# Graph attention layer: the residual's pass split in two and widened by the source terms, and the next graph's input norm one step sooner

## The reference, cut to what matters

```
h    = relu(layernorm(x))                         # input norm
Wh   = h @ W ;  src = Wh @ a[:64] ;  dst = Wh @ a[64:]
e    = leaky_relu(src[:, None] + dst[None, :], 0.2), masked where adj == 0
z    = elu(softmax(e) @ Wh + h @ W_res)           # residual term h @ W_res
out  = layernorm(z) * gamma + beta                # output norm
x    = x + out
```

## Time and profile before

| | us |
|---|---|
| median of 3 runs | 3389.66 |
| lowest, highest | 3387.86, 3393.14 |
| the profiled execution | 3394.82 |
| its span, first to last instruction | 3392.6 |

### The profile page before, as it was taken

How to read it: one execution, slowest core, us unless ns; L and a number is a source line. 1 busy time by engine, 2 the same in 40 slices (tenths; PEclk the granted TensorE clock), 3 DMA queues, 4 the chain that set the end, 5 groups by cost and what they waited for, 6 DMA issues and landing times. The chain is left out here.

```text
span 3392.6 us, 78775 instructions
## 1 busy us (share of the span) xinstructions
PE 3004.1 (89%) x30972; PEld 1659.6 (49%) x30972; DVE 3021.8 (89%) x4666; ACT 2922.6 (86%) x3806; POOL 994.7 (29%) x869
## 2 busy tenths in 40 slices
PE   7996999999999989898898898998998989886875
PEld 5764666666666633333333333333333333335764
DVE  7886898888888899999999999999999999983666
ACT  4554887888888789999999999999999999995776
POOL 4443776767767600000000000000000000004676
PEclk9997999999999999999999999999999999996898
DMA  7640000000000000000000000000000000001221
GB/s 247 222 154 20 23 25 20 23 23 21 23 20 22 17 11 11 11 11 11 11 11 11 11 11 11 11 11 11 11 10 11 9 10 11 11 7 58 60 62 47
DMA packets 68411, 111.58 MB, mean 33 GB/s; under 512 B 26452, under 2 KB 26582, under 8 KB 68054
## 3 DMA queue, kind: packets, MB, share of 16 engines
q1 hardware_dynamic: 68054, 106.69, 10.2%
HBM read 86.61 MB, written 18.87 MB: 31 GB/s over the span
## 5 line engine op out<-in xcount | busy, mean ns | idle before, releaser
L1349 ACT ACTIVATE l_scalar_ring<-l_w,l_r 128x1024 f32<-128x1024 f32 x1568 | 1651.7, 1156 | 7.1 <-PEq L322 6.7
L1389 DVE TENSOR_SCALAR l_vector_ring<-l_w_code,l_r_code 128x2048 f32<-128x2048 f32 x1264 | 1602.6, 1340 | 3.0 <-PE scores L1281 0.5
L1271 PE MATMUL scores<-l_scalar_ring,l_signs 128*32 128x512 f32 x6272 | 753.5, 598 | 79.4 <-ACT l_scalar_ring L1349 78.8
L1281 PE MATMUL scores<-l_vector_ring,l_signs_code 128*32 128x512 f16 x10112 | 683.5, 393 | 101.4 <-DVE l_vector_ring L1389 99.6
L464 POOL TENSOR_TENSOR l_masked<-l_relu,mask 128x512 f32<-128x512 f32 x512 | 585.3, 1165 | 313.9 <-ACT l_relu L699 301.3
L277 ACT ACTIVATE l_probs<-l_logits,negmax 128x1024 f32<-128x1024 f32 x384 | 441.9, 1151 | 206.5 <-DVE negmax L268 201.3
L172 POOL TENSOR_TENSOR stat<-stat,minus_half 128x8 f32<-128x8 f32 x32 | 73.2, 2288 | 1833.5 <-DVE stat L167 1833.4
L1281 PEld LDWEIGHTS scores<-l_vector_ring,l_signs_code 128*32 128x32 bf16 x10112 | 252.0, 95 | 562.4 <-DVE l_vector_ring L1389 225.0
L209 PE MATMUL turned<-ident,l_probs 128*128 128x128 f32 x3072 | 430.8, 285 | 35.7 <-ACT l_probs_t L1760 21.2
L1271 PEld LDWEIGHTS scores<-l_scalar_ring,l_signs 128*32 128x32 f32 x6272 | 185.8, 109 | 430.0 <-issue 243.9
L209 PEld LDWEIGHTS turned<-ident,l_probs 128*128 128x128 f32 x3072 | 340.7, 144 | 103.5 <-issue 97.8
(11 more groups left out here) (249 smaller groups left out, 3393.9 us busy)
## 6 DMA issues: line engine op xcount, KB each, us to landing
mask<-masks_kept SPq DMA_DIRECT2D x192, 256.0 KB, 2.6
l_adj<-adj SPq DMA_DIRECT2D x64, 512.0 KB, 5.8
masks_kept<-l_mask_ring SPq DMA_DIRECT2D x64, 256.0 KB, 4.9
x_res<-x SPq DMA_DIRECT2D x8, 256.0 KB, 4.8
out<-x_res SPq DMA_DIRECT2D x8, 256.0 KB, 2.7
l_h<-l_h SPq DMA_DIRECT2D x8, 128.0 KB, 2.8
l_kl<-l_dh SPq DMA_DIRECT2D x32, 2.0 KB, 1.7
l_kl<-l_dl SPq DMA_DIRECT2D x32, 2.0 KB, 1.7
```

What stands on the lines that cost most here:

```text
L1271: last = nc.tensor.matmul(s.scores[g * ROWS:(g + 1) * ROWS, buf, half, :], signs[:, window], scalar_ring[:, at % SCALAR_RING, g, halves[ha ...
L1281: last = nc.tensor.matmul(s.scores[g * ROWS:(g + 1) * ROWS, buf, half, :], signs_code[:, par, g % 2, window], parts(vector_ring[:, at % VE ...
L1349: last = nc.scalar.activation(scalar_ring[:, at % SCALAR_RING, g, :], w[:, par, :], ACT.Relu, bias=r[:, par, column:column + 1])
L1389: last = nc.vector.tensor_scalar(vector_ring[:, at % VECTOR_RING, g:g + 2, :], w_code[:, par, :, :], r_code[:, par, 0, column:column + 1], ...
```

## The change

Everything is in `gat_layer`.

- The residual's pass (fill k = 4) and the source terms' pass become one. `wres` gets a 65th column, W times a_src scaled by 1 - slope, and each of 8 matmuls of 65 columns gives the residual term and the source term of its 128 rows together. They are written to a part of `outT` of 4 x 65 columns, so in two halves: at n = 2 and n = 3 (`rest_of`). VectorE takes each half with a copy of 260 columns (`take_rest`) ahead of the copy to `turned_out`. ScalarE's copy at n = 4 and VectorE's `take_sources` go. K is 4.
- `take_relu` waits for the half that holds its block, and takes its bias from `rest`.
- On GpSimd the input norm of graph b+2 moves one step ahead: centre n = 2, square n = 3, power and y n = 6. `out_centre` goes from n = 6 to n = 7.
- On VectorE `out_seed` goes from n = 2 to 3, the input norm's variance from 5 to 4, elu and its mean from 4 to 5, and the values of graph b+1 from 5 to 1.
- `unit_out` moves from columns 192 to 255 of `outT` to columns 128 to 191.
- At the start of the layer the two halves of graph 0 follow each other through the same part of the bank, with VectorE's copy between them.

```diff
-    K = 5
+    K = 4
+    HALF = NB // 2
-        wres = sb("wres", [P, D], F32)
+        wres = sb("wres", [P, D + 1], F32)
-        rest = sb("rest", [P, 2, NB, D], F32)
+        rest = sb("rest", [P, 2, NB, D + 1], F32)
-        sources = s.outT[:, 3 * P:3 * P + NB]
-        unit_out = s.outT[:, P + D:P + 2 * D]
+        rest_bank = s.outT[:, P + D:P + D + HALF * (D + 1)].rearrange("p (a d) -> p a d", d=D + 1)
+        unit_out = s.outT[:, P:P + D]
...
@@ gpsimd
-                g.wait_ge(sems["fill_copied"], fills_needed(b))
+                g.wait_ge(sems["fill_copied"], b * K + K)
...
+                    if n == 2 and norm:
+                        layer_norm_centre(g, s, sems, next_norm(s, b), b + 2)
                     if n == 3 and norm:
-                        layer_norm_centre(g, s, sems, next_norm(s, b), b + 2)
-                    if n == 4 and norm:
                         layer_norm_square(g, s, sems, b + 2)
                     if n == 5 and before > 1:
                         out_scale(b - 2)
-                    if n == 6 and before > 0:
-                        out_centre(b - 1)
-                    if n == 7 and norm:
+                    if n == 6 and norm:
                         g.wait_ge(sems["values_ready"], b + 1)
                         layer_norm_apply(g, s, sems, next_norm(s, b), par, b + 2, b * K + 2)
+                    if n == 7 and before > 0:
+                        out_centre(b - 1)
@@ tensor
-            def turn_sources(b, par):
+            def rest_of(b, par, half):
                 pe.wait_ge(sems["fill_copied"], b * K + 2)
-                for j in range(NB):
-                    last = nc.tensor.matmul(sources[:, j:j + 1], hT[0:D, par, j * P:(j + 1) * P], w_src[0:D, :], start=True, stop=True,
-                                            skip_group_check=True)
+                for j in range(HALF):
+                    block = half * HALF + j
+                    last = nc.tensor.matmul(rest_bank[:, j, :], hT[0:D, par, block * P:(block + 1) * P], wres[0:D, :], start=True,
+                                            stop=True, skip_group_check=True)
...
-                    if n == 2 and project:
-                        turn_sources(b + 1, 1 - par)
+                    if n in (2, 3) and project:
+                        rest_of(b + 1, 1 - par, n - 2)
                     product(par, n, u)
...
-            turn_sources(0, 0).then_inc(sems["src_turned"], 1)
+            for half in range(2):
+                wait(pe, sems["src_ready"], half)
+                rest_of(0, 0, half).then_inc(sems["src_turned"], 1)
@@ scalar
-                a.wait_ge(sems["fill_copied"], fills_needed(b))
-                a.wait_ge(sems["src_ready"], b + 1)
+                a.wait_ge(sems["fill_copied"], b * K + K)
+                a.wait_ge(sems["src_ready"], 2 * b + 1 + n // HALF)
...
-                    for k in takes_at(n, project, (0, 1, 4)):
+                    for k in takes_at(n, project, (0, 1)):
@@ vector
-            def take_sources(par):
-                nc.vector.tensor_scalar(src[:, par, :], sources, 1.0 - SLOPE, None, ALU.mult).then_inc(sems["src_ready"], 1)
+            def take_rest(par, half):
+                nc.vector.tensor_copy(rest[:, par, half * HALF:(half + 1) * HALF, :], rest_bank).then_inc(sems["src_ready"], 1)
...
                     v.wait_ge(sems["out_ready"], u + 1)
-                    if n == 2 and project:
-                        take_sources(1 - par)
+                    if n in (2, 3) and project:
+                        take_rest(1 - par, n - 2)
                     nc.vector.tensor_copy(turned_out[:], s.outT[:, 0:P]).then_inc(sems["out_copied"], 1)
                     for k in takes_at(n, project, (2, 3)):
                         take_fill(b + 1, 1 - par, k)
...
-                    if n == 2 and before > 1:
+                    if n == 1 and project:
+                        take_values(b + 1, 1 - par)
+                    if n == 3 and before > 1:
                         out_seed(b - 2)
-                    if n == 4 and before > 0:
+                    if n == 4 and norm:
+                        layer_norm_scale(v, s, sems, next_norm(s, b), b + 2)
+                    if n == 5 and before > 0:
                         elu_sum(b - 1, 1 - par)
                         out_mean(b - 1)
-                    if n == 5 and norm:
-                        layer_norm_scale(v, s, sems, next_norm(s, b), b + 2)
-                    if n == 5 and project:
-                        take_values(b + 1, 1 - par)
...
-            nc.vector.tensor_copy(w_src[0:D, :], s.outT[0:D, P:P + 1]).then_inc(sems["weights_ready"], 1)
+            nc.vector.tensor_scalar(wres[0:D, D:D + 1], s.outT[0:D, P:P + 1], 1.0 - SLOPE, None, ALU.mult).then_inc(sems["weights_ready"], 1)
...
-            v.wait_ge(sems["src_turned"], 1)
-            take_sources(0)
+            for half in range(2):
+                v.wait_ge(sems["src_turned"], half + 1)
+                take_rest(0, half)
```

More of the change, by code:

```diff
@@ L1519, in gat_layer @@
         w_dst = sb("w_dst", [P, P], F32)
-        w_src = sb("w_src", [P, 1], F32)
         hT = sb("hT", [P, 2, N], F32)
         dst_slope = sb("dst_slope", [P, 2, N], F32)
-        src = sb("src", [P, 2, NB], F32)
         values = sb("values", [P, 2, NB, D], F32)
@@ L1551, in _ @@
             sp.wait_ge(sems["weights_ready"], 1)
-            for to, at in ((w[0:D, :], w_dram), (w[D:P, :], w_dram), (wres[0:D, :], w_res),
+            for to, at in ((w[0:D, :], w_dram), (w[D:P, :], w_dram), (wres[0:D, 0:D], w_res),
                            (acol[0:D, 0:1], a_dram[0:D].rearrange("(d a) -> d a", a=1)),
@@ L1578, in _ @@
             sp.wait_ge(sems["stored"], 16 * B)
-        def fills_needed(b):
-            return K if isinstance(b, int) and b == 0 else b * K + 4
         @block.gpsimd
@@ L1663, in fill @@
                     last = turn_y(pe, s, par, k, bank)
-                elif k < 4:
+                else:
                     last = nc.tensor.matmul(bank[:], w_dst[0:D, :], hT[0:D, par, cols], start=True, stop=True)
-                else:
-                    for j in range(NB):
-                        last = nc.tensor.matmul(bank[:, j * D:(j + 1) * D], hT[0:D, par, j * P:(j + 1) * P], wres[0:D, :],
-                                                start=True, stop=True, skip_group_check=True)
                 last.then_inc(sems["fill_ready"], 1)
-            def turn_sources(b, par):
+            def rest_of(b, par, half):
                 pe.wait_ge(sems["fill_copied"], b * K + 2)
-                for j in range(NB):
-                    last = nc.tensor.matmul(sources[:, j:j + 1], hT[0:D, par, j * P:(j + 1) * P], w_src[0:D, :], start=True, stop=True,
-                                            skip_group_check=True)
+                for j in range(HALF):
+                    block = half * HALF + j
+                    last = nc.tensor.matmul(rest_bank[:, j, :], hT[0:D, par, block * P:(block + 1) * P], wres[0:D, :], start=True,
+                                            stop=True, skip_group_check=True)
                 return last
@@ L1723, in _ @@
                 fill(0, 0, k)
-            turn_sources(0, 0).then_inc(sems["src_turned"], 1)
+            for half in range(2):
+                wait(pe, sems["src_ready"], half)
+                rest_of(0, 0, half).then_inc(sems["src_turned"], 1)
             turn_probs(pe, s, sems, probs[:, 0, :], 0)
-            pe.wait_ge(sems["src_ready"], 1)
+            pe.wait_ge(sems["src_ready"], 2)
             graph(0, 0, True, first=True)
@@ L1741, in take_fill @@
                 a.wait_ge(sems["fill_ready"], b * K + k + 1)
[L1742 to L1745, removed]
+                last = nc.scalar.activation(hT[0:D, par, cols], bank[0:D, :], ACT.Relu)
                 last.then_inc(sems["fill_copied"], 1)
             def take_relu(b, par, n):
-                a.wait_ge(sems["fill_copied"], fills_needed(b))
-                a.wait_ge(sems["src_ready"], b + 1)
+                a.wait_ge(sems["fill_copied"], b * K + K)
+                a.wait_ge(sems["src_ready"], 2 * b + 1 + n // HALF)
                 wait(a, sems["logits_ready"], STARTS + b * NB + n - 1)
-                nc.scalar.activation(relu[n % 2], dst_slope[:, par, :], ACT.Relu, bias=src[:, par, n:n + 1],
+                nc.scalar.activation(relu[n % 2], dst_slope[:, par, :], ACT.Relu, bias=rest[:, par, n, D:D + 1],
                                      scale=1.0 / SLOPE - 1.0).then_inc(sems["relu_ready"], 1)
@@ L1788, in graph @@
                         elu_power(b - 1)
-            for k in (0, 1, 4):
+            for k in (0, 1):
                 take_fill(0, 0, k)
@@ L1841, in finish @@
                 nc.vector.scalar_tensor_tensor(out=z[:, par, n, :], in0=unit_out, scalar=s.rinv[:, slot:slot + 1],
-                                               in1=rest[:, par, n, :], op0=ALU.mult, op1=ALU.add
```

(3 more changed lines are left out.)

## The result

The changed kernel takes 3362.21 us (median of 4 runs, 3359.71 to 3367.33) against 3391.4 (median of 4, 3387.86 to 3397.2) of the kernel before: ratio 0.9914, interval 0.9895 to 0.9933. Measured again on two other chips it was 0.9916 (0.9899 to 0.9934) and 0.9907 (0.9891 to 0.9923). The forecast was 3375.4 and the range ended at 3365: the direction was right, the gain, 29 us, was twice what was forecast. It is the size of the rival in which the clock comes free (-27). Of the 33.3 us between the two profiled spans (3392.6 and 3359.3), 30.4 lie in the last layer, from its first load on; the other 2.9 lie ahead of it, where the change touches nothing.

What follows compares the result with a forecast made beforehand. In graphs 2 to 5 the loop of dst, GpSimd's list, y and step 0 was taken to bound. Graphs 2 to 5 -9.6, passes -2.2, start -2.5: -14.3 us, 3375.4 for the median; range 3365 to 3387.

Steps and rivals of the forecast that it cites:

- the rival in which the clock comes free: No half clock in graphs 1 to 5, less in the others and the start: -27 us, 3362.7; chance 0.12.
- the half clock: TensorE at 1.2 GHz lengthens the period of graphs 2 to 5; 2.0 us taken for each.
- the low end: Bound of the term for graphs 2 to 5: no half clock at all, -17.5 us instead of -9.6.
- the price of 0.4 per us: From graph 1: 5.5 us of lost time for 13.6 us of TensorE half clock.
- The row that I held against the low end: Trace window where TensorE's clock falls to 0.57 although it is busy 4.00 of 4 us.
- It is low after the waits for y: Trace reading: TensorE's clock is low after its waits for GpSimd's y, four of them, 11.2 us in all.
- The full-clock period: Graphs 2 to 5, without added half clock: 14.3 + 16.8 + 1.3 = 32.4 us per graph.
- The new wait for the mask of step 7: VectorE's `logit` of step 0 waits for GpSimd's mask, now behind y: 0.9 us per graph.
- The passes: Joining two TensorE passes shortens steps 1 to 5 in graphs 0, 1 and 6: 0.75 us each, -2.2 in all.
- The start: Start of the layer: sources complete sooner, first `logit` earlier on VectorE: -2.5 us, ends -1.5 and -4.8.
- The end: Graph 7 and behind it, same operations but `out_seed` and elu a step later: 0, give or take 0.7 us.
- the slower rival: TensorE's clock in all seven periods makes every graph like graph 1: +12.6 us, 3402.3; chance 0.05.

Runs made afterwards that it cites:

- e8_source64: The kernel before with the source pass as 16 matmuls of 64 columns instead of 1: 3386.60 us, ratio 0.9980 against before.
- e11_order_again: The kernel before with only the GpSimd and VectorE order changed, passes not joined, second run: 3375.41 us, ratio 0.9933 against before.
- e10_order64: The kernel before with the change of order and a 64-column source pass: 3367.09 us, ratio 0.9916 against before.
- e2_join: The changed kernel with both engines' old order put back, passes still joined: 3383.41 us, ratio 0.9965 against before.
- e0_after: The changed kernel itself, measured again on another chip: 3363.37 us, ratio 0.9916 against the kernel before.
- e13_after_again: The changed kernel itself, measured again on the chip of the order runs: 3364.94 us, ratio 0.9907 against the kernel before.

## Why the prediction was wrong

**The step that failed is the half clock**, "I take 2.0" a graph, and with it the bound: I called the low end (no half clock) unlikely on the strength of the earlier trace rows. Measured 6.4, 13.8 and 6.4 us in three profiles of the changed kernel, in sum over seven graphs, where the price of 0.4 per us makes 0.4 to 0.8 a graph. That price holds for long spells: e8_source64 ran graph 1 in 32.18 us at the full clock, 5.7 less than before for 13.6 us of half clock, and graph 4 of e11_order_again paid 9.7 for 23.8. The row that I held against the low end was the right row read too narrowly: TensorE was full in 3144 to 3148, but it came out of the 1-column pass (start 3142.59), which the change removes. e10_order64 shows that this pass lowers the clock, and e2_join that long waits for y do the same (0.91 in each of graphs 3 to 5); the change takes away both causes. "It is low after the waits for y" was itself true of two of the four.

The Trainium skill (TensorE: Matmul & The Clock Gate, "What's actually happening") says that activity releases the throttle. The long waits agree with it: after 3.78 us of idle TensorE ran at the low clock. The pass does not: there the clock fell with TensorE 1.00 of 1.00 us busy. The free clock, which that rule would give, is what came; but part of it came by taking away a pass in which TensorE was busy, so that rival was right in size and named only a part of the cause.

**The full-clock period** was forecast at 32.4 us and measured at 31.65 to 32.42 in graphs 2 to 5. Inside it, y came 13.3 us after dst instead of 14.3, since the first two masks took 4.51 for 5.08, scaling 1.04 for 1.45 and the power 1.64 for 2.09 (y itself 1.33 for 1.05). The new wait for the mask of step 7 did not show. What bounds instead seems to be a mixture of TensorE in steps 1 to 3 and VectorE's work ahead of `finish` in steps 3 to 7 (32 waits, 32.4 us); no run takes the two apart.

**The passes**: 1.00 us a half (forecast 1.0), the copy 0.43 (0.41), step 1 to 2 5.34 (5.31 by the same account). Step 2 to 3 came out at 4.31, 0.9 more than before where I gave "most of 0.98". In graph 0 the steps from 1 to 4 take 12.1 us instead of 13.3; in graph 6, where I forecast -0.75, they take 13.4 as before, and the graph became 1.2 longer. The clock isn't the reason: in e0_after graph 6 takes 31.57 us at the full clock, and with the order alone (e11_order_again) 31.23, against 30.60 before. The join is worth little on its own work: 2.1 us between e10_order64 and e13_after_again, and by the profiles it lies in the start (38.95 and 35.69 us from the first load to the first copy), for graphs 0 to 6 add up to 219.34 and 219.17. At the full clock it costs 0.5 us in each of graphs 2 to 5 (graph 4: 31.39 and 31.86) and gains 0.5 to 0.7 in graphs 0 and 1. What it gave beyond that it gave through the clock.

**The start**: from the copy of the weights' row (`a_rows`, 3073.19 and 3070.66) to the first `logit` 18.36 and 16.06 us, -2.3 where -2.5 was forecast. **The end**: +0.7, at its bound.

**The account.** Between the profiles the layer became 30.4 us shorter. The 34.6 us less of half clock are worth some 14 of them at 0.4 (an estimate); the sum had 1.2 there, 0.3 in each of four graphs. The other 16 to 17 are waits for y, passes and start, where the sum had 13.1. So of the 16 us that the forecast missed, the clock is some 13 and the rest 3. The rival "clock comes free" had the right size with a chance of 0.12.

Small slips in the working change nothing of this: without half clock four graphs would give 4 x (36.84 - 32.4) = 17.8, not 17.5; the list up to y adds up to 14.5, not 14.3; and the slower rival gives graph 0 the whole length of graph 1 (+6.0) and not only its half clock (+4.2 at 0.4).

What stays open: why half clock strikes some graphs and not others of equal work (graph 4 of e11_order_again, 23.8 us of it, graph 3 none), and why an added pass of 60 columns brings it at later waits. The runs show that the narrow pass and the waits move it, not the full condition, and each rests on one profile a run.

## What to carry to other kernels

When the granted clock dips while TensorE shows busy, look at what it ran just before. Here it was a row of 16 matmuls of 1 column; widening it with columns that nobody reads returned 8.3 us for 0.35 us of longer passes in seven graphs (0.05 each), and joining it with a wider pass took the falls at this place away too. When a change removes a long wait of TensorE, count the half clock behind it as part of the wait: in the kernel before it followed the waits of 3.78 and 3.89 us and not those of 1.21 and 2.33. And where a queue is blocked at one point, as GpSimd was for 5.47 us at the mask of step 4, work put ahead of that point is free, while all behind it delays the last of the list.

## What the runs showed that I had not expected

Sixteen float32 matmuls with 64 x 128 weights take 1.84 us with 1 column and 1.89 with 64: the width costs 0.05 us a pass, and saved 8 us of 3375 through the clock. A pass of 1.84 us added in seven graphs cost 34 us, more than half of it through half clock, a good part of which begins 8 us and more behind the pass, at waits that the kernel has without the pass too.
